# A new order of work in the ramp of a gated two-block layer

## The reference, cut to what matters

```
kv[b,i,j,:] = ctx[b,i,:] * ctx[b,j,:]              # 8 x 8 products, symmetric in i, j
y   = causal_convolution(kv, ssm_kernel[head]) + kv * D[head]
att[b,j,:]  = sum_i y[b,i,j,:] * layernorm(x)[b,i,:]
x   = x + tanh(g_xattn) * att
```

## Time and profile before

| | us |
|---|---|
| median of 3 runs | 872.45 (870.46 to 872.83) |
| the profiled execution's own time | 872.01 |
| its span in the profile | 870.2 |
| busy: TensorE / DVE / POOL / ACT | 826.7 / 732.2 / 643.6 / 438.3 |

### The profile page before, as it was taken

One profiled execution on the slowest core, in us unless ns is written; L12 is line 12 of the kernel. 1 busy time (PEld: TensorE's weight loads), 2 busy tenths in 40 slices (PEclk: granted clock), 3 DMA queues, 4 the chain that ended last, 5 costly groups with the idle time before them and its releaser, 6 DMA issues.

```text
span 870.2 us, 17260 instructions
## 1 busy us (share of the span) xinstructions
PE 826.7 (95%) x6208; PEld 691.8 (80%) x6208; DVE 732.2 (84%) x1489; ACT 438.3 (50%) x941; POOL 643.6 (74%) x579
## 2 busy tenths in 40 slices
PE   3889999999999999999999999999999999999973
PEld 2768888888888888888888888888888888888862
DVE  5798888889888898988889899888888988889842
ACT  3564555555555545545555554555555555554330
POOL 6668778778877787797778778877877887776331
PEclk9798999999999999999999999999999999999996
DMA  8401222012222211222221122222112222210000
GB/s 244 146 3 54 67 68 51 24 60 69 67 68 67 63 26 47 67 69 68 67 68 37 34 66 68 67 68 68 48 25 62 68 68 67 68 50 13 2 14 23
DMA packets 26676, 51.78 MB, mean 59 GB/s; under 512 B 3232, under 2 KB 4640, under 8 KB 26592
## 3 DMA queue, kind: packets, MB, share of 16 engines
q1 hardware_dynamic: 22320, 46.19, 19.5%
q10 hardware_dynamic: 4272, 4.48, 1.6%
HBM read 42.12 MB, written 8.55 MB: 58 GB/s over the span
## 4 chain that ended last, share of the span: by engine, by line
PE 87%; issue 3%; POOL 1%; DVE 1%; POOLq 0%; ACT 0%; DVEq 0%; ACTq 0%
PE bank L333 39%; PE bank L304 25%; PE bank L285 10%; PE bank L370 4%; PE bank L385 4%; PE bank L317 2%; PE bank L293 2%; PE bank L320 1%; PE bank L443 0%; POOL rstd L710 0%; POOLq L68 0%; POOL o_rstd L710 0%; DVE y_raw L848 0%; POOL rot_b L739 0%; DVE x L992 0%
## 5 line engine op out<-in xcount | busy, mean ns | idle before, releaser
L304 PE MATMUL bank<-kv_pair,toep 128*128 128x512 f32 x960 | 244.8, 401 | 1.0 <-DVE z_terms L838 1.0
L304 PEld LDWEIGHTS bank<-kv_pair,toep 128*128 128x128 f32 x960 | 175.3, 190 | 41.0 <-DVE z_terms L838 7.5
L704 POOL TENSOR_TENSOR kv_pair<-kv,kv_pair 128x576 fp32r<-128x576 f32 x126 | 178.1, 1425 | 6.2 <-ACT kv_pair L536 2.8
L695 POOL TENSOR_TENSOR kv<-kx 128x512 f32<-128x512 f32 x128 | 160.5, 1254 | 5.5 <-DMA kx<-in_ctx 4.1
L710 POOL TENSOR_TENSOR o_rstd<-o_ve,minus_half 128x16 f32<-128x16 f32 x32 | 93.2, 2911 | 78.4 <-DVE o_ve L924 78.4
L848 DVE TENSOR_REDUCE y_raw<-z_terms 128x128 f32<-128x1024 f32 x128 | 149.2, 1204 | 0.0
L710 POOL TENSOR_TENSOR rstd<-ve,minus_half 128x1 f32<-128x1 f32 x64 | 39.2, 612 | 120.3 <-DVE ve L1003 117.3
L333 PE MATMUL bank<-w_all_high,yT_high 128*128 128x512 f32 (+2 forms) x512 | 119.6, 355 | 0.0
L333 PE MATMUL bank<-w_all_low,yT_high 128*128 128x512 f32 (+2 forms) x512 | 111.7, 340 | 0.0
L333 PE MATMUL bank<-w_all_high,yT_low 128*128 128x512 f32 (+2 forms) x512 | 106.1, 339 | 0.0
L536 ACT ACTIVATE kv_pair<-kv 128x576 fp32r<-128x576 f32 x128 | 87.2, 682 | 20.6 <-POOL kv L698 19.7
(11 more groups left out here) (108 smaller groups left out, 1517.5 us busy)
## 6 DMA issues: line engine op xcount, KB each, us to landing
toep<-taps_dram SPq DMA_DIRECT2D x31, 512.0 KB, 7.0
kx<-in_ctx SPq DMA_DIRECT2D x32, 384.0 KB, 7.5
x_in<-in_x SPq DMA_DIRECT2D x32, 256.0 KB
out_x<-out_sb SPq DMA_DIRECT2D x32, 256.0 KB
wv_t<-in_L_ffn_Wv ACTq DMA_DIRECT2D x1, 1024.0 KB, 8.5
w_g<-in_L_ffn_Wg ACTq DMA_DIRECT2D x1, 1024.0 KB, 6.9
w_out<-in_L_ffn_Wout ACTq DMA_DIRECT2D x1, 1024.0 KB, 9.9
w_qk<-in_L_ffn_Wq ACTq DMA_DIRECT2D x1, 512.0 KB, 4.6
```

The costliest lines, as they stand in the source:

```text
L304: ins = nc.tensor.matmul(bank[lc % 2][:, :], toep[:, 1 - p, a, (lc - mc) * P:(lc - mc + 1) * P], kv_p[b][:, 1 - p, mc, 0:FULL], start=(mc ...
L695: eng.tensor_tensor(view(kv[:, c % 2, 0:FULL], [[ROW, NROT], [1, ROW]]), view(kx[:, p, c, 0:ROW], [[0, NROT], [1, ROW]]), view(kx[:, p, c, ...
L704: eng.tensor_tensor(kv_p[1][:, p, c, :], kv[:, c % 2, :], kv_p[0][:, p, c, :].bitcast(F32), ALU.subtract).then_inc(kv_ready[c], 1)
```

## The change

- Products 0 and 1 of head 0 and the low part of product 0 are made by DVE; POOL has the low parts of 1, 2 and 3 (DVE had 2 and 3), all in step -2.
- `split_taps_low` and `output_weights_low` move from DVE to POOL; the first runs at the end of step -2, the second in step 0 behind products 2 and 3. ACT rounds the taps after qn and not before it. A wait for `taps_ready` is added ahead of the sums of head 0.
- v's weights are made in four pieces: 0 and 1 at the end of step -1, 2 and 3 within step 0; their roundings and low parts are spread over step -1 and step 0, and the wait for `v_low` is split. The banks are in another order.
- g's weights are rounded in step -1 and subtracted behind the first two sums of step 0; q's and k's are rounded earlier and subtracted after a wait for `rstd2_ready`.
- Head 1's roundings 0 and 1 move behind qn, product 2's behind extend, product 3's into step 0. POOL waits for `mul_last` before head 1's products.
- `d_first` and `anti` are loaded by ACT's queue, first of all, and not SP's. The loads of q's and k's weights are issued ahead of the first Toeplitz rounding; those of gates, conv_w, Wg and Wout at the end of step -2.
- DVE zeroes z at the start, TensorE multiplies the zeros six times (results unused), and ACT does one silu of one column.

The diff without context, by engine:

Semaphore, banks and SyncE's queue:

```diff
@@ -185,0 +186 @@
+        z_zeroed = sem("z_zeroed")
@@ -228 +229 @@
-        V_BANKS = (4, 5, 6, 3)
+        V_BANKS = (6, 3, 4, 5)
@@ -240,2 +240,0 @@
-            eng.dma_start(anti, consts[:, C_ANTI:C_ANTI + P]).then_inc(s_raw, 16)
-            eng.dma_start(d_first, ssm_D[0:1].rearrange("(a n) -> a n", a=1).partition_broadcast(P)).then_inc(s_raw, 16)
```

TensorE:

```diff
@@ -349 +348 @@
-            def prepare_value_weights():
+            def prepare_value_weights(c):
@@ -351,5 +350,9 @@
+                for d in range(CH):
+                    ins = nc.tensor.matmul(bank[V_BANKS[c]][:, d * P:(d + 1) * P], wv_t[:, d, c * P:(c + 1) * P],
+                                           prep[:, 0:P], start=True, stop=True)
+                ins.then_inc(v_w_ps, 1)
+            def keep_busy(ps, n):
+                for _ in range(n):
+                    nc.tensor.matmul(ps[:, :], z[:, 0:P], z[:, :], start=True, stop=True)
@@ -356,0 +360,2 @@
+            eng.wait_ge(z_zeroed, 1)
+            keep_busy(bank[6], 6)
@@ -409,0 +415,2 @@
+                    if h == 0:
+                        prepare_value_weights(2)
@@ -423,0 +431,2 @@
+                    if h == 0:
+                        prepare_value_weights(3)
@@ -427 +436 @@
-                        eng.wait_ge(v_low, CH)
+                        eng.wait_ge(v_low, 2)
@@ -451,0 +461,2 @@
+                    else:
+                        eng.wait_ge(v_low, CH)
@@ -475 +486,2 @@
-                    prepare_value_weights()
+                    prepare_value_weights(0)
+                    prepare_value_weights(1)
```

ScalarE:

```diff
@@ -497,0 +510,2 @@
+            eng.dma_start(d_first, ssm_D[0:1].rearrange("(a n) -> a n", a=1).partition_broadcast(P)).then_inc(s_raw, 16)
+            eng.dma_start(anti, consts[:, C_ANTI:C_ANTI + P]).then_inc(s_raw, 16)
@@ -502,0 +517,3 @@
+            eng.wait_ge(z_zeroed, 1)
+            eng.activation(nmr1[:, :], z[:, 0:1], ACT.Silu)
@@ -550 +567,4 @@
-                if pre:
+                if h == 0:
+                    kv_round(1, 3, 1)
+                    round_value_weights(1)
+                if pre and h != -1:
@@ -554,2 +573,0 @@
-                    eng.wait_ge(raw_d, 1)
-                    eng.activation(toep[:, 0, 0, :], toep_raw, ACT.Copy).then_inc(toep_high, 1)
@@ -565,2 +582,0 @@
-                    eng.wait_ge(taps_d, 1)
-                    eng.activation(taps_p[0:NH, 0, :], taps[0:NH, :], ACT.Copy).then_inc(taps_high, 1)
@@ -568,0 +585,2 @@
+                    eng.wait_ge(raw_d, 1)
+                    eng.activation(toep[:, 0, 0, :], toep_raw, ACT.Copy).then_inc(toep_high, 1)
@@ -587,0 +606,4 @@
+                if h == -1:
+                    round_weights(0, 2 * DK, w_qk, s_wqk, 2, qk_high)
+                    eng.wait_ge(s_gates, 48)
+                    eng.activation(gates[:, :], gates[:, :], ACT.Tanh).then_inc(gates_ready, 1)
@@ -589 +611,2 @@
-                    round_weights(G0, DV, w_g, s_wg, 1, g_high)
+                    round_value_weights(2)
+                    round_value_weights(3)
@@ -615,4 +638,2 @@
-                        eng.dma_start(gates[:, 0:1], g_xattn.rearrange("(a n) -> a n", a=1).partition_broadcast(P)
-                                      ).then_inc(s_gates, 16)
-                        eng.dma_start(gates[:, 1:2], g_ffn.rearrange("(a n) -> a n", a=1).partition_broadcast(P)
-                                      ).then_inc(s_gates, 16)
+                        eng.wait_ge(taps_d, 1)
+                        eng.activation(taps_p[0:NH, 0, :], taps[0:NH, :], ACT.Copy).then_inc(taps_high, 1)
@@ -620,2 +641,2 @@
-                        eng.wait_ge(s_gates, 48)
-                        eng.activation(gates[:, :], gates[:, :], ACT.Tanh).then_inc(gates_ready, 1)
+                        kv_round(p, 0, h + 2)
+                        kv_round(p, 1, h + 2)
@@ -623,3 +644 @@
-                        round_weights(0, 2 * DK, w_qk, s_wqk, 2, qk_high)
-                        kv_round(p, 2, h + 2)
-                        kv_round(p, 3, h + 2)
+                        round_weights(G0, DV, w_g, s_wg, 1, g_high)
@@ -631,4 +650,3 @@
-                    if first_step:
-                        eng.dma_start(w_conv[:, :, :], conv_w.rearrange("(c p) k -> p c k", p=P)).then_inc(s_gates, 16)
-                        eng.dma_start(w_g[:, :, :], Wg.rearrange("(c p) n -> p c n", p=P)).then_inc(s_wg, 16)
-                        eng.dma_start(w_out[:, :, :], Wout.rearrange("(c p) n -> p c n", p=P)).then_inc(s_wout, 16)
+                    if h == -1:
+                        kv_round(p, 2, h + 2)
+                        round_value_weights(0)
@@ -666,0 +685,8 @@
+                if first_step:
+                    eng.dma_start(gates[:, 0:1], g_xattn.rearrange("(a n) -> a n", a=1).partition_broadcast(P)
+                                  ).then_inc(s_gates, 16)
+                    eng.dma_start(gates[:, 1:2], g_ffn.rearrange("(a n) -> a n", a=1).partition_broadcast(P)
+                                  ).then_inc(s_gates, 16)
+                    eng.dma_start(w_conv[:, :, :], conv_w.rearrange("(c p) k -> p c k", p=P)).then_inc(s_gates, 16)
+                    eng.dma_start(w_g[:, :, :], Wg.rearrange("(c p) n -> p c n", p=P)).then_inc(s_wg, 16)
+                    eng.dma_start(w_out[:, :, :], Wout.rearrange("(c p) n -> p c n", p=P)).then_inc(s_wout, 16)
@@ -675,3 +700,0 @@
-                if h == -1:
-                    for c in range(CH):
-                        round_value_weights(c)
```

GpSimd (the two functions are the same as before, on another engine):

```diff
@@ -707,0 +731,12 @@
+            def split_taps_low():
+                eng.wait_ge(taps_high, 1)
+                eng.tensor_tensor(taps_p[0:NH, 1, :], taps[0:NH, :], taps_p[0:NH, 0, :].bitcast(F32), ALU.subtract
+                                  ).then_inc(taps_ready, 1)
+            def output_weights_low():
+                eng.wait_ge(wout_high, 1)
+                eng.tensor_tensor(w_out_p[1][:, :, :], w_out[:, :, :], w_out_p[0][:, :, :].bitcast(F32), ALU.subtract
+                                  ).then_inc(wout_low, 1)
@@ -716 +751,2 @@
-                if pre:
+                    eng.wait_ge(mul_last, 1)
+                if pre and h != -2:
@@ -719,3 +754,0 @@
-                if h == -2:
-                    rsqrt(rstd1, ve1, 1, ve1_ready, h + 3, rstd1_ready)
-                if pre:
@@ -722,0 +756 @@
+                if pre:
@@ -723,0 +758,2 @@
+                if h == -2:
+                    rsqrt(rstd1, ve1, 1, ve1_ready, h + 3, rstd1_ready)
@@ -749,0 +786,2 @@
+                if h == 0:
+                    output_weights_low()
@@ -753,3 +791,4 @@
-                    if h != -2:
-                        kv_rest(p, 2, h + 2)
-                        kv_rest(p, 3, h + 2)
+                    kv_rest(p, 2, h + 2)
+                    kv_rest(p, 3, h + 2)
+                if h == -2:
+                    split_taps_low()
```

VectorE:

```diff
@@ -760,0 +800,12 @@
+            eng.memset(z[:, :], 0.0).then_inc(z_zeroed, 1)
+            def first_products(c):
+                if c == 0:
+                    eng.wait_ge(s_kx[0], 16)
+                eng.tensor_tensor(view(kv[:, c, 0:FULL], [[ROW, NROT], [1, ROW]]),
+                                  view(kx[:, 0, c, 0:ROW], [[0, NROT], [1, ROW]]),
+                                  view(kx[:, 0, c, 0:ROW], [[NB, NROT], [1, ROW]]), ALU.mult)
+                eng.tensor_tensor(kv[:, c, FULL:FULL + HALF], kx[:, 0, c, 0:HALF],
+                                  kx[:, 0, c, HALF:2 * HALF], ALU.mult).then_inc(kv_made[c], 1)
@@ -767,6 +817,0 @@
-            def split_taps_low():
...
-            def output_weights_low():
...
@@ -847,0 +887,2 @@
+                else:
+                    eng.wait_ge(taps_ready, 2)
@@ -897,2 +937,0 @@
-                if setup_step:
-                    first_rest(2)
@@ -910,2 +948,0 @@
-                if setup_step:
-                    first_rest(3)
@@ -917,0 +955,3 @@
+                if h == 0:
+                    value_weights_low(1)
+                    value_weights_low(2)
@@ -929,0 +970,4 @@
+                if h == -2:
+                    first_products(0)
+                    first_products(1)
+                    first_rest(0)
@@ -934 +977,0 @@
-                    split_taps_high()
@@ -936 +979 @@
-                    split_taps_low()
+                    split_taps_high()
@@ -949 +992 @@
-                    weights_low(G0, DV, w_g, g_high, g_low)
+                    value_weights_low(3)
@@ -958,0 +1002,2 @@
+                if h == 0:
+                    weights_low(G0, DV, w_g, g_high, g_low)
@@ -1008,0 +1054 @@
+                    eng.wait_ge(rstd2_ready, 1)
@@ -1010,2 +1056 @@
-                    for c in range(CH):
-                        value_weights_low(c)
+                    value_weights_low(0)
@@ -1013 +1057,0 @@
-                    output_weights_low()
```

More of the change, by code:

```diff
@@ L347, in prepare_logit_weights @@
                 ins.then_inc(logit_w_ps, 1)
-            def prepare_value_weights():
-                for c in range(CH):
```

(26 more changed lines are left out.)

## The result

The changed kernel takes 890.41 us (median of 4 runs, 889.08 to 892.9); the kernel before, run beside it, 872.08 (4 runs, 870.46 to 872.83). The ratio is 1.021, 95% interval 1.0196 to 1.0224: **18 us slower**, where I had forecast 869.5 and a range up to 872.2. The profiled execution took 891.29 us, its span is 889.5 (before 870.2).

A forecast was written before the change was run, and what follows sets the result against it. TensorE was taken as the bound from the second step on, so only the ramp could gain: 2.3 us at the second z's transposes plus 0.2 from the clock, 872.0 - 2.5 = 869.5 us, range 865.8 to 872.2.

The forecast's parts named there:

- The step that failed: From the second step on TensorE is the bound, untouched by the diff; a ramp gain carries to the end one for one.
- the port's rule: DVE operations with two SBUF inputs and POOL operations exclude each other; whichever starts first blocks the other for its whole instruction.
- Rival B: End of step 0: POOL starts w_out's low part too late; slower than before from 57.8, 873.3 us at 59; chance 0.10.
- a different period than before between 100 and 800 us: A sign that the forecast is wrong, in the steady steps; no size or chance of its own.
- The ramp's own terms: Estimates up to the second z's transposes, which were to start at 66.2 instead of 68.47: 2.3 us gained.
- Step -2: Ramp: earlier loads and products split between DVE and POOL; qn 9.8 to 10.6, last convolution at 17.6 against 20.98.
- The zeroed products: TensorE's six zeroed fp32 matmuls at the start: 8.6 us taken, ending between 4.2 and 9.8, ahead of qn.
- Step -1: Ramp: z of head 0 ends at 31.5 instead of 38.97, 7.4 us earlier.
- Step 0: Gain partly given back: projections 42.9, 3.4 us earlier; signed copy, blocked by POOL's w_out low part, ends 61.3, 1.2 earlier.
- rival A: End of step 0: signed copy not blocked, ends 58.3; transposes gain 4 to 5.5 us, 866 in all; chance 0.22.

The follow-up runs named there:

- experiment 6: The kernel of experiment 4 with w_out's low part still on POOL but moved behind rstd2: 870.27 us, ratio 0.9968.
- experiment 7: The kernel of experiment 4 with w_out's low part moved back to DVE, behind a wait for rstd2: 868.07 us, ratio 0.9951.
- experiment 4: The changed kernel with POOL waiting for both last products (mul_last) before its first rotation rot_a: 871.91 us, ratio 0.9985.
- experiments 1 and 9: The kernel before with one-column memsets of an unused tile at the head of DVE's program: three in the first, 894.24 us; 67 in the second, 896.05 us.
- the two best kernels: Experiment 7's kernel, 868.04 us when repeated, and the kernel before with POOL's wait for mul_last ahead of rot_a alone, 868.7 us when repeated.
- experiments 4, 6 and 8: The last of these: the kernel of experiment 4 without TensorE's six zeroed matmuls and their wait, 871.5 us, ratio 0.9981.
- experiment 2: The changed kernel with four one-column memsets more at the head of DVE's program: 872.27 us, ratio 0.9991.

## Why the prediction was wrong

**The step that failed** is the first, on which everything else stood: "from the second step on, TensorE is the bound and nothing of the diff touches it", and so a gain "is carried to the end one for one". TensorE was at 25.91 of 26 us, but DVE's signed copy reached it with only 0.12 us to spare. I took DVE's 22.41 of 26 us as slack. A delay of 0.33 us on it brought 1.10 more with it, and TensorE lost all of the sum, 20.33 us over 29 steps. The diff did touch the loop: not its instructions but their numbers. I had the port's rule, and I had the first of the two last products at 0.43 in the earlier trace rows against 1.51 in the earlier trace rows. What I didn't look at is by how much it was 0.43: its successor starts only 0.03 us ahead of POOL's rot_a. No sum over the ramp's edits could show this.

**The rivals.** None named it. Rival B had the sign, with a mechanism in the ramp that would have shown the transposes late; they came 0.88 us early. My last sentence named "a different period than before between 100 and 800 us" as what nothing allowed for. That was the sign of what happened, but no chance and no part of the range was given to it: I priced that event at zero, and slower in all at 0.07.

**The ramp's own terms.** I had forecast 2.3 us at the transposes; 0.88 came.
- Step -2: rows of after against my numbers. The zeroed products took 7.65 us and ended at 9.10 (8.6 and 9.8): right. kx landed later, so the first product began at 5.60 and not 4.95, and qn at 11.56, not 9.8; the last convolution began at 19.13 instead of 17.6. I had also d_tap leave earlier; its addition came at 13.96, where I had 12.4 and before had 11.77. Of the loads, d_first did land sooner after its issue (4.5 us, before 6.7), but first_toeplitz then waited for the kernel's taps (8.3 us, before 5.6) and came at 10.32, before at 9.71; kx took 7.6 (5.7) and d_tap 10.0 (7.1).
- Step -1: z ended at 32.60 (forecast 31.5) and projections began at 43.76 (42.9). The gains against 38.97 and 46.30 are 6.4 and 2.5 us where I had 7.4 and 3.4: each is one microsecond short, no more than the 1.5 lost in step -2.
- Step 0: the signed copy started 0.52 us behind POOL's w_out low part and was blocked until its end, as forecast, not at 0.68 as in rival A. Timeline of DVE after, then of POOL:

```profile
...
58.28 4.53 DVE L898 SCALAR_TENSOR_TENSOR qke<-qke,u 128x512 f32<-128x512 f32 x1
```

```profile
...
57.76 4.50 POOL L740 TENSOR_TENSOR w_out_low<-w_out,w_out_high 128x2048 fp32r<-128x2048 f32 x1
64.83 0.55 POOL L745 TENSOR_TENSOR rstd<-ve,minus_half 128x1 f32<-128x1 f32 x1 [2.57 <-DVE ve L1048]
```

It ended at 62.81 and not 61.3, since POOL began at 57.76 and not 55.5. That start lies at rival B's break-even, 57.8. rstd2 fell from 2.61 to 0.55 as forecast, z ended at 67.13 (65.1), and the transposes at 67.59 were held by the scores (65.57 + 2.09), not by z, also as forecast (66.2). Experiments 6 and 7 show this part's price: with the low part out of the copy's way the transposes come 3.4 and 5.6 us sooner than in experiment 4.

Two slips in the working change nothing: 26.0 + 5.3 is 31.3 and not 31.5, and the signed copy before ended at 61.88 + 0.68 = 62.56 and not at 62.48.

So in this part the mechanisms were right, and the sizes were some 1.4 us too good. It is the smaller error, 1.4 of 21 us.

**What stays open.** What DVE does in its pause isn't in the trace; shown are its length, its period and that the number of instructions ahead of it decides where it falls. Whether it also occurs in the kernel before isn't shown. I had supposed that POOL's chain hides it there; but the trace shows it at no place of DVE, where odd and even steps have the same starts to 0.04 us, so if it occurs, it lies behind DVE's own work. The step of 26.81 us had a pause 0.02 us longer than the others (0.45 and not 0.43 from o_ve to the gated product). There the first of the two last products lost the race with rot_a as well and took 1.58. In experiments 1 and 9 it is the same; why that pause is longer is open. And which of the two best kernels is faster isn't settled.

## What to carry to other kernels

An engine with 12% of idle time can still set the pace: read, for each thing that the bounding engine takes from it, how long before its use it is ready (here 0.83 us for one, 0.12 for another), and delay it by a tenth of a microsecond in an experiment before taking that time as free. Where two engines exclude each other and the order is a matter of timing, read by how much the right one wins; if it is by hundredths, write the order down as a wait (here one wait, 0.9954 on the kernel before, and 0.9985 where the unprotected one had 1.021). A change of setup code moves the numbers of all later instructions: compare the period of the steady loop, not only the point up to which the edited part reaches. That holds for experiments too: one that moves an operation to another engine also moves the count there, as experiment 7 did.

## What the runs showed of the hardware

- DVE paused for 0.25 to 0.27 us once in 128 of its instructions, seen as idle time with the releaser "issue" (the instruction starts 0.33 to 0.35 us later than without it): 14 times in each of the changed kernel, the kernels with 3 and 67 instructions more and experiments 4, 6 and 8, always ahead of instruction 320, 448 and so on, and at no place to be seen with 4 more than the changed kernel. The number of instructions from the start of the program decides where it falls.
- A long POOL operation blocks a DVE operation with two SBUF inputs that starts behind it (0.68 became 4.53 us), and DVE's holds up POOL's (0.55 became 2.61). Who starts first has it: 0.03 us decide over 1.1 us in every step.
- The clock's low level (0.50) late in the run differs between profiles in place and in length: the mean is 0.79 in 828 to 836 us before and 0.58 in experiment 2, 0.57 in 820 to 828 us in experiment 7, and 1.00 through 820 to 844 us in experiment 6. The last distance between marks is 21.89, 23.19, 23.20 and 20.62 us in these four.
